# One strided maximum over 18 tiles in place of a halving and a maximum over 9

## The reference: what is computed

```python
h_edge = ((atom[src] + bond) @ W).reshape(-1, H, D)
h_node = (atom @ W).reshape(-1, H, D)
el = jnp.einsum('ehd,hd->eh', h_edge, attn_l)
er = jnp.einsum('nhd,hd->nh', h_node, attn_r)
s = el + er[dst]
s = jnp.where(s > 0, s, NEG_SLOPE * s)
smax = jax.ops.segment_max(s, dst, num_segments=N)
ex = jnp.exp(s - smax[dst])
denom = jax.ops.segment_sum(ex, dst, num_segments=N)
alpha = ex / denom[dst]
ft = jax.ops.segment_sum(h_edge * alpha[..., None], dst, num_segments=N)
h = ft.mean(axis=1)
```

## Time and profile before

| | us |
|---|---|
| median of 3 runs | 9480.21 |
| lowest and highest | 9476.06 and 9481.56 |
| the profiled execution | 9480.92 |
| its span, first to last instruction | 9479.2 |

### The profile page before, as it was taken

The page is one execution under the profiler, slowest core; times in us unless marked ns, Lnnn a source line. Parts: engine busy times, 40 slices in busy tenths (PEclk is TensorE's granted clock), DMA queues, the critical chain, the costliest instruction groups (busy, mean ns, idle before and its releaser), DMA issues. The chain is left out here.

```text
span 9479.2 us, 125330 instructions
## 1 busy us (share of the span) xinstructions
PE 4772.3 (50%) x23674; PEld 4371.0 (46%) x23674; DVE 7034.2 (74%) x11845; ACT 4623.3 (49%) x12210; POOL 6767.6 (71%) x6888
## 2 busy tenths in 40 slices
PE   4677777777634444444444444444444444444434
PEld 4666666666623444444443444444443333333333
DVE  2788888888747777777776777777776777777777
ACT  1677777777614444444443444444443444444443
POOL 0777777777507777777776777777776777777776
PEclk9666666666655555555555555555555555555555
DMA  1222222222211111111111111111111111111111
GB/s 41 57 56 55 54 56 56 55 54 57 51 56 31 31 31 31 31 31 31 31 31 27 31 31 31 31 31 31 31 31 28 32 32 33 32 33 32 32 32 30
DMA packets 675574, 360.05 MB, mean 38 GB/s; under 512 B 549773, under 2 KB 550477, under 8 KB 675022
## 3 DMA queue, kind: packets, MB, share of 16 engines
q0 software_dynamic: 220896, 237.06, 13.3%
q1 hardware_dynamic: 454626, 122.45, 6.3%
HBM read 335.55 MB, written 23.35 MB: 38 GB/s over the span
## 5 line engine op out<-in xcount | busy, mean ns | idle before, releaser
L1323 POOL DMA_INDIRECT plain_rows_in<-table,plain_idx x5139 | 4965.9, 966 | 1590.7 <-issue 1590.7
L1571 PE MATMUL plain_ps_sums<-plain_rows_in,plain_prob 128*125 x10908 | 2435.1, 412 | 7.7 <-ACT plain_prob L1534 7.7
L1571 PEld LDWEIGHTS plain_ps_sums<-plain_rows_in,plain_prob 128*125 128x125 f32 x10908 | 2374.8, 329 | 33.2 <-ACT plain_prob L1534 8.3
L789 POOL DMA_INDIRECT heads_rows_in<-h_in,heads_idx x1713 | 1782.5, 1041 | 532.5 <-issue 532.5
L1534 ACT ACTIVATE plain_prob<-plain_prob 128x2250 f32<-128x2250 f32 x300 | 623.6, 2079 | 1845.3 <-DVE plain_prob L1459 1845.3
L1592 PE MATMUL plain_ps_max<-ident,plain_column_max 128*125 128x128 f32 x300 | 173.0, 577 | 2530.0 <-DVE plain_column_max L1440 2530.0
L1592 PEld LDWEIGHTS plain_ps_max<-ident,plain_column_max 128*125 128x125 f32 x300 | 85.2, 284 | 2606.5 <-DVE plain_column_max L1440 2606.5
L1525 ACT ACTIVATE plain_score_sb<-plain_mask,plain_rows_in 128x125 f32<-128x125 f32 x1800 | 553.8, 386 | 1318.8 <-DMA plain_rows_in<-table,plain_idx 1318.8
L1434 DVE TENSOR_TENSOR plain_top<-plain_score_sb,plain_ps_score 128x750 f32<-128x750 f32 x300 | 280.9, 936 | 1149.5 <-ACT plain_ps_score L1525 1145.9
L1525 ACT ACTIVATE plain_ps_score<-plain_mask,plain_rows_in 128x125 f32<-128x125 f32 x3600 | 1059.0, 347 | 0.0
L1019 ACT ACTIVATE heads_masked<-heads_mask,heads_scores_sum 128x125 f32<-128x125 bf16 x3600 | 1052.1, 385 | 2.4 <-DVE heads_scores_sum L854 2.1
(11 more groups left out here) (240 smaller groups left out, 7604.2 us busy)
## 6 DMA issues: line engine op xcount, KB each, us to landing
plain_rows_in<-table,plain_idx POOLq DMA_INDIRECT x5139, 2.4
heads_edges<-in_edge_attr SPq DMA_DIRECT2D x104, 544.0 KB
heads_rows_in<-h_in,heads_idx POOLq DMA_INDIRECT x1713, 2.4
plain_own<-table SPq DMA_DIRECT2D x312, 32.7 KB
table<-plain_out_sb SPq DMA_DIRECT2D x200, 32.7 KB
n_x<-in_x SPq DMA_DIRECT2D x2, 3125.0 KB
plain_unit_int<-unit_ints SPq DMA_DIRECT2D x312, 0.0 KB
plain_idx<-in_src SPq DMA_DIRECT2D x312, 8.5 KB
```

Of the source, the lines that this page charges most:

```text
L789: gp.indirect_dma_start(rows_in[h][:, t, :], None, table[:, :], bass.IndirectOffsetOnAxis(ap=idx[h][:, t:t + 1], axis=0)).then_inc(done, 16)
L1323: gp.indirect_dma_start(rows_in[h][:, t, :], None, table[:, :], bass.IndirectOffsetOnAxis(ap=idx[h][:, t:t + 1], axis=0)).then_inc(done, 16)
L1571: ins = te.matmul(sums[h % 2], prob[h % 2][:, t, :], rows, start=t == 0, stop=t == Q - 1)
```

## The change

`head_max` of the heads layer no longer takes the elementwise maximum of tiles 0 to 8 and 9 to 17 into a buffer `top` and reduces that over 9 tiles. It reduces over all 18 tiles of `masked` in one instruction. The input is read with the tile index innermost, a stride of 125 floats, as the reduction before read `top`. The buffer goes, and the number of chained VectorE steps in a unit falls from 24 to 22.

```diff
     PARTS = 3
-    HALF = Q // 2
     PAIRS = Q // 2
...
         masked = sb("masked", [P, heads, Q, NB])
-        top = sb("top", [P, HALF, NB])
         column_max = sb("column_max", [P, heads, NB])
...
                 rounds = unit_rounds(ve)
-                STEPS = 24
+                STEPS = 22
...
                     ve.wait_ge(masked_made, heads * n + hd + 1)
-                    step(ve.tensor_tensor(top[:, :, :], masked[:, hd, 0:HALF, :], masked[:, hd, HALF:Q, :], ALU.max))
-                    step(ve.tensor_reduce(column_max[:, hd, :], top[:, :, :].rearrange("p t n -> p n t"), AX.X,
-                                          ALU.max))
+                    step(ve.tensor_reduce(column_max[:, hd, :], masked[:, hd, :, :].rearrange("p t n -> p n t"),
+                                          AX.X, ALU.max))
                     ve.sem_inc(columns_maxed, 1)
```

## The result

The changed kernel takes 9537.73 us (median of 4 runs, 9536.65 to 9539.95), against 9480.0 for the kernel before: ratio 1.0062, 95% interval 1.0044 to 1.0079. That is 58 us more; 9529, +49, was predicted. Its profiled execution took 9538.61 us round a span of 9536.8.

What follows compares the result with a forecast made beforehand. The bound was taken to be the heads layer's ring of ScalarE masks, TensorE turns and scores, and VectorE logits, not GpSimd. Terms 14 + 41 - 6 = +49 us gave 9529 us, own range 9515 to 9550, with rivals 9482 to 9568.

Steps and rivals of the forecast that it cites:

- The sum: Heads layer's losses less the gathers' gain: 14 + 41 - 6 = +49 us, giving 9529 us.
- The price: Each head's new reduction of 2250 elements costs 4.35 us, at L872's 1.867 ns an element; chance 0.50.
- L555's: Rival price for the new reduction, from a stride of 64 floats: 3.90 us, +1 us; 0.10 for 3.9 or lower.
- Growth before the turn: Both heads' maxima grow 0.74 us each, 1.47 us a unit, ahead of TensorE's turn of the column maxima.
- The first room: Between the second maximum's end and TensorE's turn: hides 0.63 us in 62 units, 0.37 us in 37.
- The second room: VectorE's idle before L923, behind TensorE's scoring: hides another 0.62 us in 62 units, nothing in 37.
- Gathers: GpSimd gets faster with L871 gone, so VectorE's waits for gathered rows after the start go: -6.4 us.
- The two kinds: Heads units: 62 at TensorE's low clock lose 0.22 us each, 14 us; 37 at high clock 1.10, 41 us.
- The clock: Rival: all units at TensorE's low clock, +10 us more; 0.09 for worse clock or a reduction dearer than 4.40 us.

Runs made afterwards that it cites:

- The probe: Kernel before with 17 pairs of maxima of various counts and strides put ahead of the heads layer's loop; 12248.91 us in one execution, on a slow chip.
- gathers16_b: Kernel before with one of the 17 gathers of each heads unit left out; 9493.19 us against 9498.66, ratio 0.9994.
- two half-size experiments: stride128 and one_head_b, each measured against the kernel before at 9498.66 us: +21 and +20 us.
- stride128: Changed kernel with masked scores stored 128 floats apart from tile to tile; 9519.79 us against 9498.66 for the kernel before, ratio 1.0022.
- one_head_b: Changed kernel with head 1 back to its halving and reduction, only head 0 by one strided instruction; 9519.05 us against the kernel before's 9498.66, ratio 1.0025.
- tile_inner: Changed kernel with masked scores stored tile index innermost, reduced contiguously; 12319.96 us against the kernel before's 12230.42 on a slow chip, total not used.
- tree_b: Kernel before with each head's maximum by five elementwise maxima and no reduction; 9586.46 us, ratio 1.0095.

## Why the prediction was right

The forecast moved the right way for the reason given: VectorE's maxima grew, two rooms hid a part, and the rest was paid. The sum was 9 us short, from terms that were wrong by more than that and partly made up for each other. Its points in turn:

- **The price.** 4.35 predicted by L872's own row, 4.356 measured. The probe shows why that row was the right one and L555's not: the stride, 500 bytes against 256, sets the price, and neither the count of terms nor of outputs does.
- **Growth before the turn.** 1.47 a unit predicted. In the mean of 99 units the second maximum ends 15.10 us after L854 before and 16.54 after L852: 1.44.
- **The first room.** Its mean was 0.57 us before and is 0.11 after, so 0.46 was hidden, 45 us in 99 units. I had 62 x 0.63 + 37 x 0.37 = 53: the turn follows its maximum by 0.11 us and not by the 0.05 that I took from the plain layer.
- **The second room.** From L918's end to L923 the mean went from 0.28 to -0.11, so 0.39 was hidden, 38 us, as predicted (62 x 0.62 = 38).
- **What I left out.** Short VectorE instructions got longer (below): 0.08 us a unit from L894 to the end of the weighting and 0.06 in the logits, 14 us. I had put this at nothing.
- **Gathers.** Waits for rows fell from 24.3 us to 17.9: -6.4 us, as predicted. In gathers16_b too they are gone, without another gain that its time would show.
- **The sum** of the measured parts for a unit: 1.44 - 0.46 - 0.39 + 0.14, less 0.02 in the turn itself and 0.13 from the logits to the next L854 (half of it the waits for rows), is 0.59 before rounding; times 99, 58.7 us.
- **The two kinds.** The score matmuls ran at the high clock (granted 0.8 or more) in 37 of 99 units before and at 0.50 in the other 62, just those in which L923 waited. Each unit compared with itself, the 37 lost 1.15 us each, 42.6 in all, where 1.10 and 41 were predicted, and the 62 lost 0.26 each, 16.0 in all, where 0.22 and 14 were. The first room hid 0.36 and 0.51 us in them, the second nothing and 0.62.
- **The clock.** After the change only 15 units scored at the high clock; 31 of the 37 had fallen and 9 others had risen. The sum had no term for this; among the rivals it stood with +10 us if all units fell. The 15 take 23.47 us, the others 23.73: a lead of 0.26, where 0.27 was predicted. So the 22 units fewer cost about 22 x 0.26 = 6 us, which is part of the losses above. Why the clock fell in them no run tells.

The two half-size experiments missed by more, +20 for +8 and +21 for +4. Their traces, against that of the kernel before on the other chip, give these reasons:

- **stride128.** From the first L852 to the last there are 2306.9 us, +20.5. Its score matmuls ran at the high clock in 16 units and not in 37. The 56 units that kept their level changed by nothing in sum, 32 that fell lost 0.83 us each, 26.6 in all, and 11 that rose gained 6.2. So the miss is the clock, which the expectation took as unchanged: units at the high clock take 22.87 us there and the others 23.39. In gathers16_b, on the same chip, 35 units are high, so the chip alone doesn't explain it; whether the edit lowered the clock was not tested.
- **one_head_b.** Its heads layer grew by only 10.1 us (2296.5), near the 8 expected, 29 units being high. The profiled execution, 9514.6 us, was the fastest of its ten, and the rest of the +20 lies outside what this trace shows.

## What to carry to other kernels

An engine that never pauses need not be the bound: look whether anyone waits for it, then take a piece of its work away. Price a longer instruction by the row with the same stride, and count the growth against the idle time behind each hand-over in turn; what is hidden differs from unit to unit when TensorE's clock does. A saving ahead of a wait is worth nothing, and the same time added there is free only up to that wait.

## What the runs showed of the hardware

**A strided reduction's price depends on the exact stride**: 1.04 ns an element when contiguous (rows, and 2.50 us for 2250 elements in tile_inner), 1.67 at 16, 32, 64 and 128 floats, 1.76 to 1.79 at 4, 8, 68, 72, 124 and 132, 1.86 to 1.88 at 125 and 126 (the probe's rows). Padding a row of 125 floats to 128 took the reduction from 4.36 to 3.99 us in stride128.

**Short VectorE instructions end with a gather.** L927 of the changed kernel (L930 before) takes 0.18 us, or up to 0.38. Two units where it is long and one where it is short, and then the gathers beside the two long ones and a gather after a pause:

```profile
1020.31 0.36 DVE L927 TENSOR_SCALAR heads_logits<-heads_logits 128x36 f32<-128x36 f32 x1
1045.72 0.37 DVE L927 TENSOR_SCALAR heads_logits<-heads_logits 128x36 f32<-128x36 f32 x1
1068.65 0.18 DVE L927 TENSOR_SCALAR heads_logits<-heads_logits 128x36 f32<-128x36 f32 x1
```

```profile
1019.72 0.94 POOL L787 DMA_INDIRECT heads_rows_in<-h_in,heads_idx  x1 [0.30 <-issue]
...
1045.14 0.94 POOL L787 DMA_INDIRECT heads_rows_in<-h_in,heads_idx  x1 [0.30 <-issue]
...
1058.95 0.94 POOL L787 DMA_INDIRECT heads_rows_in<-h_in,heads_idx  x1 [4.60 <-issue]
```

The long ones end at 1020.67 and 1046.09, the gathers at 1020.66 and 1046.08. In 63 of 100 units after the change it was longer than 0.18 us, each time ending with a gather; before in 21. Where a gather still had 0.3 to 0.4 us to run when L927 began, it took 0.35 to 0.38 us (54 units), and with 0.2 to 0.3 us to run 0.23 (9 units); with 0.6 to 0.7 us to run it took 0.18 (26 units), as with no gather beside it (11). The cast L898 too gets longer beside a gather. Their means, after and then before:

```profile
L927 DVE TENSOR_SCALAR heads_logits<-heads_logits 128x36 f32<-128x36 f32 x100 | 28.6, 286 | 3.4
...
L898 DVE CAST heads_node_split<-heads_node_vals 125x4 bf16<-125x4 f32 x100 | 24.1, 240 | 3.5
```

```profile
L930 DVE TENSOR_SCALAR heads_logits<-heads_logits 128x36 f32<-128x36 f32 x100 | 21.8, 218 | 3.4
...
L901 DVE CAST heads_node_split<-heads_node_vals 125x4 bf16<-125x4 f32 x100 | 19.8, 198 | 3.5
```

The `tensor_tensor` between them (L925 after, L928 before) took 202 and 196 ns in the mean and never over 240. The Trainium skill has the pattern, SBUF — State Buffer, "Who interferes with whom": copies, casts and `tensor_scalar` may take the port pair that GpSimd uses, and whoever comes first holds it for its whole instruction. The rows agree on who waits, with up to 0.2 us an instruction, but not on the whole: a gather with more than half of its 0.94 us still to run did not hold L927. So GpSimd's gathers lengthen VectorE's short instructions as VectorE's two-input ones lengthen gathers, and how often depends on how the two loops fall against each other. That the shift of the loops made it more frequent here is read from the traces, not tested. The last gather row is one of GpSimd's new pauses, 4.60 us.

**A loop's turn can cost 3 to 4 us, with instructions loaded meanwhile**: 4.2 us in the median in tree_b and 3.2 in the probe's kernel, 0.55 in the kernel before, with 159 packets in the queue `q14 instruction` against 38 (the rows are with tree_b). The probe's kernel has no instruction more in its loop.
